# Centring the FFN matrix along its rows, taking the first normalisation's factors for two tiles at once, and moving the residual ahead of them on Pool

## The reference, cut to what matters

```
xn    = LN(x) * gamma + beta
gate  = sigmoid(xn @ w_gate + b_gate)
delta = sigmoid(xn @ w_delta + b_delta);   B = xn @ w_in + b_in
h_t   = tanh((h_{t-1} * delta_t) @ A + B_t)          # 2048 steps, state of 16
y     = (h @ C) * gate + x
x1    = LN(x + y)
out   = LN(x1 + real(ifft(fft(x1) @ w)) + bias)
```

## Time and profile before

| | us |
|---|---|
| median of three runs | 955.33 (955.02 to 956.43) |
| the profiled execution | 954.58 |
| its span, first to last instruction | 952.8 |
| PE busy | 919.6 (97%) |
| DVE busy | 755.5 (79%) |
| ACT busy | 561.2 (59%) |
| POOL busy | 515.0 (54%) |
| mean granted TensorE clock | 0.998 |

### The profile page before, as it was taken

One profiled execution on the slowest core, in us unless ns is written; L12 is line 12 of the kernel. 1 busy time (PEld: TensorE's weight loads), 2 busy tenths in 40 slices (PEclk: granted clock), 3 DMA queues, 4 the chain that ended last, 5 costly groups with the idle time before them and its releaser, 6 DMA issues.

```text
span 952.8 us, 19703 instructions
## 1 busy us (share of the span) xinstructions
PE 919.6 (97%) x5748; PEld 513.0 (54%) x5748; DVE 755.5 (79%) x1616; ACT 561.2 (59%) x1047; POOL 515.0 (54%) x1313
## 2 busy tenths in 40 slices
PE   6999999999999999999989999999999999999996
PEld 3555555555555555556775555454545454545453
DVE  6988788887888878888578887878787878787874
ACT  2533333333333333345474788888888888888887
POOL 1422222222222222232217888888888888888884
PEclk9999999999999999999999999999999999999999
DMA  9444455444554445532406576676766666767653
GB/s 328 137 141 146 156 176 176 137 149 155 176 176 137 147 157 176 176 133 93 174 1 174 179 248 233 223 244 223 235 222 240 224 238 221 238 225 239 223 176 133
DMA packets 89483, 175.84 MB, mean 185 GB/s; under 512 B 3057, under 2 KB 5361, under 8 KB 89458
## 3 DMA queue, kind: packets, MB, share of 16 engines
q1 hardware_dynamic: 89024, 175.00, 55.0%
q10 hardware_dynamic: 434, 0.54, 0.2%
HBM read 106.45 MB, written 67.11 MB: 182 GB/s over the span
## 4 chain that ended last, share of the span: by engine, by line
PE 48%; POOL 34%; issue 8%; DVE 5%; ACT 1%; DMA 1%; POOLq 1%; DVEq 0%
POOL x_sb L676 12%; PE bank L1164 12%; PE bank L1167 12%; PE bank L1165 12%; POOL rstd L634 7%; PE bank L1154 6%; POOL rnorm L700 4%; POOL scaled_mean L683 2%; POOL veps L632 2%; PE bank L1209 2%; PE bank L1188 1%; POOL lift_bias L686 1%; POOL rstd L702 1%; POOL nbias L704 1%; PE bank L1191 1%
## 5 line engine op out<-in xcount | busy, mean ns | idle before, releaser
L913 DVE SCALAR_TENSOR_TENSOR lo_sb<-bank,hi_sb 128x512 f16<-128x512 f32 x256 | 176.7, 690 | 84.0 <-ACT hi_sb L443 65.0
L443 ACT ACTIVATE hi_sb<-bank 128x512 f16<-128x512 f32 x128 | 76.4, 597 | 263.8 <-PE bank L1154 263.8
L632 POOL TENSOR_TENSOR veps<-mv,c_eps 128x1 f32<-128x1 f32 x256 | 49.4, 193 | 315.3 <-DVE mv L894 315.3
L1164 PE MATMUL bank<-z_sb,hi_sb 128*128 128x512 f16 x512 | 193.8, 379 | 9.3 <-DVE w_ring L1085 8.2
L1164 PE MATMUL bank<-wg_hi,hi_sb 128*128 128x512 f16 x512 | 194.0, 379 | 1.6 <-ACT hi_sb L443 0.8
L1165 PE MATMUL bank<-wg_lo,hi_sb 128*128 128x512 f16 x512 | 194.0, 379 | 0.0
L1165 PE MATMUL bank<-z_sb,hi_sb 128*128 128x512 f16 x512 | 193.9, 379 | 0.0
L676 POOL TENSOR_TENSOR x_sb<-x_sb,gate_sb 128x512 f32<-128x512 f32 x128 | 163.5, 1277 | 12.1 <-DVE gate_sb L1073 11.3
L1154 PE MATMUL bank<-cst,norm_sb 128*128 128x128 f32 x1024 | 158.7, 278 | 10.0 <-DVE norm_sb L907 8.2
L634 POOL TENSOR_TENSOR rstd<-veps,c_half 128x1 f32<-128x1 f32 x256 | 139.6, 545 | 20.1
L1079 DVE BATCH_NORM_STATS2 bn<-x_sb 128x6 f32<-128x512 f32 x128 | 88.5, 691 | 67.7 <-POOL x_sb L676 67.6
(11 more groups left out here) (158 smaller groups left out, 1215.9 us busy)
## 6 DMA issues: line engine op xcount, KB each, us to landing
x_sb<-x SPq DMA_DIRECT2D x63, 1024.0 KB, 6.9
gate_dram<-gate_sb SPq DMA_DIRECT2D x32, 1024.0 KB, 5.4
gate_sb<-gate_dram SPq DMA_DIRECT2D x32, 1024.0 KB, 5.3
out<-out_sb SPq DMA_DIRECT2D x31, 1024.0 KB, 5.3
h_rep<-fourier_constants SPq DMA_DIRECT2D x2, 514.0 KB, 12.8
x_sb<-x SPq DMA_DIRECT2D x2, 512.0 KB, 6.5
w_ring<-w_gate SPq DMA_DIRECT2D x2, 512.0 KB, 6.3
w_re_sb<-w_freq_real SPq DMA_DIRECT2D x1, 1024.0 KB, 12.2
```

The source lines that it names most:

```text
L913: nc.vector.scalar_tensor_tensor(lo_sb[:, k % 2].rearrange("p t r -> p (t r)"), ps_t[k % 2][:], ROW_SCALE, hi_sb[:, k % 2].rearrange("p t ...
L1164: nc.tensor.matmul(dst, hi_sb[:, k % 2, t], w_hi[:, t], start=(t == 0), stop=False)
```

## The change

M is centred along its rows: `combine` also takes the row sums of the last four tiles (two accumulators), makes from them `m_shift`, minus the row mean, and `high_m` and `low_m` add it. With such an M the FFN product of any row sums to zero, so the mean of `w_ring` is the mean of `norm_sb`, which is LIFT. `minus_mean`, `wsum` and `negmu` go; `squares` takes the constant -LIFT as its bias (both scaled by 1/sqrt(D)) and waits for `ffn_sum`; `scale_and_bias` has three instructions. The bound for M's scale is doubled. The first normalisation's factors are made for two tiles at once, in every odd slot, in two-column instructions, and the residual of n+5 stands ahead of them in POOL's slot.

```diff
@@ combine
+                if q < 2 * KT:
+                    ... (as before)
+                else:
+                    sums = m_sums[:, q - 2 * KT]
+                    nc.vector.scalar_tensor_tensor(dst[:, 0:HALF], odd[:, 0:HALF], ratio[sign], even, ALU.mult,
+                                                   ALU.add, accum_out=sums[:, 0:1])
+                    wait_own(nc.vector.scalar_tensor_tensor(
+                        dst[:, HALF:D], odd[:, HALF - 2:0:-1], ratio[-sign], even[:, HALF - 2:0:-1], ALU.mult,
+                        ALU.add, accum_out=sums[:, 1:2]))
+                    nc.vector.sem_inc(done, 1)
+                    nc.vector.tensor_scalar(m_shift[:, q - 2 * KT:q - 2 * KT + 1], sums[:, 0:1], sums[:, 1:2],
+                                            -1.0 / D, ALU.add, ALU.mult).then_inc(s_mshift, 1)
@@ high_m, low_m
-                act.wait_ge(s_pair, 2 * KT + i + 1)
-                nc.scalar.activation(m_hi[:, i], m_sb[:, i], ACT.Copy).then_inc(s_m_hi, 1)
+                act.wait_ge(s_mshift, i + 1)
+                nc.scalar.activation(m_hi[:, i], m_sb[:, i], ACT.Identity,
+                                     bias=m_shift[:, i:i + 1]).then_inc(s_m_hi, 1)
-                nc.vector.tensor_tensor(m_lo[:, i], m_sb[:, i], m_hi[:, i],
-                                        ALU.subtract).then_inc(s_msplit, 1)
+                nc.vector.scalar_tensor_tensor(m_lo[:, i], m_sb[:, i], m_shift[:, i:i + 1], m_hi[:, i], ALU.add,
+                                               ALU.subtract).then_inc(s_msplit, 1)
@@ ScalarE: b_normalise waits for the pair, squares for ffn_sum
-                act.wait_ge(s_blift, n + 1)
+                act.wait_ge(s_blift, v * 4 + k // 2 + 1)
-                act.wait_ge(s_negmu, n + 1)
+                act.wait_ge(s_w, n + 1)
-                nc.scalar.activation(gsum_sb[:, k % 2], w_ring[:, k], ACT.Square, bias=negmu[:, k:k + 1],
+                nc.scalar.activation(gsum_sb[:, k % 2], w_ring[:, k], ACT.Square, bias=c_squares[:],
+                                     scale=1.0 / float(np.sqrt(D)),
                                      accum_out=vsum[:, k:k + 1]).then_inc(s_sq, 1)
@@ GpSimd
+            def normalise_factors(m, k):
+                c = slice(k % 4, k % 4 + 2)
+                pool.wait_ge(s_baggr, m * 2 + 2)
+                pool.tensor_tensor(veps[:, c], mv[:, c, 1], c_eps4[:], ALU.add).then_inc(s_bveps, 1)
+                pool.wait_ge(s_bveps, m + 1)
+                pool.tensor_tensor(rstd[:, c], veps[:, c], c_half[:], ALU.pow).then_inc(s_brstd, 1)
+                pool.wait_ge(s_brstd, m + 1)
+                pool.tensor_tensor(scaled_mean[:, c], mv[:, c, 0], rstd[:, c], ALU.mult).then_inc(s_bmr, 1)
+                pool.wait_ge(s_bmr, m + 1)
+                pool.tensor_tensor(lift_bias[:, c], c_lift[:], scaled_mean[:, c],
+                                   ALU.subtract).then_inc(s_blift, 1)
-            def minus_mean(n, k):
...
@@ GpSimd, scale_and_bias
-                pool.tensor_tensor(rnorm2[:, c], var2[:, c], c_half[:], ALU.pow).then_inc(s_rnorm2, 1)
-                pool.wait_ge(s_rnorm2, m + 1)
-                pool.tensor_tensor(rstd2[:, c], rnorm2[:, c], c_rootd[:], ALU.mult).then_inc(s_rstd2, 1)
+                pool.tensor_tensor(rstd2[:, c], var2[:, c], c_half[:], ALU.pow).then_inc(s_rstd2, 1)
-                pool.tensor_tensor(nbias2[:, c], negmu[:, c], rstd2[:, c], ALU.mult).then_inc(s_nb2, 1)
+                pool.tensor_tensor(nbias2[:, c], c_neglift[:], rstd2[:, c], ALU.mult).then_inc(s_nb2, 1)
@@ GpSimd, slot of the second pass
-                if exists(n + 3):
-                    rstd_of(n + 3, (k + 3) % 8, s_baggr, s_bveps, s_brstd, c_eps4)
-                    lifted_bias(n + 3, (k + 3) % 8)
-                if exists(n - 2):
-                    minus_mean(n - 2, (k - 2) % 8)
                 if exists(n + 5):
                     residual(n + 5, (k + 5) % 8, v if k < 3 else v + 1)
+                if k % 2 == 1 and exists(n + 3):
+                    normalise_factors(v * 4 + (k + 3) // 2, (k + 3) % 8)
                 if k % 2 == 0 and exists(n - 4):
                     scale_and_bias(v * 4 + k // 2 - 2, (k - 4) % 8)
@@ VectorE
                 wait_own(nc.vector.tensor_reduce(bias_max[:], fbias_sb[:], AX.X, ALU.max, ...))
+                wait_own(nc.vector.tensor_scalar(bias_max[:], bias_max[:], 2.0, None, ALU.mult))
@@ ffn_sum
                 nc.vector.scalar_tensor_tensor(w_ring[:, k], ps_g[k % 2][:], unscale[:, 3:4],
-                                               norm_sb[:, k % 4], ALU.mult, ALU.add,
-                                               accum_out=wsum[:, k:k + 1]).then_inc(s_w, 1)
+                                               norm_sb[:, k % 4], ALU.mult, ALU.add).then_inc(s_w, 1)
```

More of the change, by code:

```diff
@@ L167, in build @@
         lift_bias = sb("lift_bias", [P, 4])
-        c_lift = sb("c_lift", [P, 1])
+        c_lift = sb("c_lift", [P, 2])
         c_eps = sb("c_eps", [P, 1])
-        c_eps4 = sb("c_eps4", [P, 1])
+        c_eps4 = sb("c_eps4", [P, 2])
         c_half = sb("c_half", [P, 2])
-        wsum = sb("wsum", [P, 8])
-        negmu = sb("negmu", [P, 8])
+        m_sums = sb("m_sums", [P, KT, 2])
+        m_shift = sb("m_shift", [P, KT])
+        c_neglift = sb("c_neglift", [P, 2])
+        c_squares = sb("c_squares", [P, 1])
         vsum = sb("vsum", [P, 8])
         var2 = sb("var2", [P, 8])
-        rnorm2 = sb("rnorm2", [P, 8])
         rstd2 = sb("rstd2", [P, 8])
-        c_mean = sb("c_mean", [P, 1])
-        c_epsd = sb("c_epsd", [P, 2])
-        c_rootd = sb("c_rootd", [P, 2])
+        c_eps2 = sb("c_eps2", [P, 2])
         nbias2 = sb("nbias2", [P, 8])
@@ L265, in build @@
         s_msplit = sem("m_split")
+        s_mshift = sem("m_centred")
         s_high = sem("scan_high_half")
@@ L295, in build @@
         s_w = sem("b_w")
-        s_negmu = sem("b_negmu")
         s_sq = sem("b_squares")
         s_var2 = sem("b_var2")
-        s_rnorm2 = sem("b_rnorm2")
         s_rstd2 = sem("b_rstd2")
@@ L580, in b_hi, with b_normalise @@
                                      scale=ROW_SCALE).then_inc(s_bhi, 1)
-            def b_normalise(n, k):
-                act.wait_ge(s_blift, n + 1)
+            def b_normalise(n, k, v):
+                act.wait_ge(s_blift, v * 4 + k // 2 + 1)
                 if before(n, 4):
@@ L608, in slot @@
                 if exists(n + 2):
-                    b_normalise(n + 2, (k + 2) % 8)
+                    b_normalise(n + 2, (k + 2) % 8, v if k < 6 else v + 1)
                 if exists(n - 5) and not (isinstance(n, int) and n - 5 == TILES - 1):
@@ L620, in _ @@
             pool.memset(c_eps4[:], LN_EPS / 4)
-            pool.memset(c_mean[:], -1.0 / D)
+            pool.memset(c_neglift[:], -LIFT)
+            pool.memset(c_squares[:], -LIFT / float(np.sqrt(D)))
             pool.memset(c_lift[:], LIFT)
-            pool.memset(c_epsd[:], LN_EPS * D)
-            pool.memset(c_rootd[:], float(np.sqrt(D)))
+            pool.memset(c_eps2[:], LN_EPS)
             pool.memset(c_half[:], -0.5).then_inc(s_pool_const, 1)
@@ L677, in residual @@
                                    gate_sb[:, k // 4, k % 4], ALU.add).then_inc(s_v, 1)
[L679 to L685, removed]
+            def normalise_factors(m, k):
[7 more added lines that the diff above has]
+                pool.wait_ge(s_bmr, m + 1)
                 pool.tensor_tensor(lift_bias[:, c], c_lift[:], scaled_mean[:, c],
                                    ALU.subtract).then_inc(s_blift, 1)
-            def minus_mean(n, k):
-                pool.wait_ge(s_w, n + 1)
-                pool.tensor_tensor(negmu[:, k:k + 1], wsum[:, k:k + 1], c_mean[:],
-                                   ALU.mult).then_inc(s_negmu, 1)
             def scale_and_bias(m, k):
@@ L697, in scale_and_bias @@
                 pool.wait_ge(s_sq, m * 2 + 2)
-                pool.tensor_tensor(var2[:, c], vsum[:, c], c_epsd[:], ALU.add).then_inc(s_var2, 1)
+                pool.tensor_tensor(var2[:, c], vsum[:, c], c_eps2[:], ALU.add).then_inc(s_var2, 1)
                 pool.wait_ge(s_var2, m + 1)
-                pool.tensor_tensor(rnorm2[:, c], var2[:, c], c_half[:], ALU.pow).then_inc(s_rnorm2, 1)
-                pool.wait_ge(s_rnorm2, m + 1)
-                pool.tensor_tensor(rstd2[:, c], rnorm2[:, c], c_rootd[:], ALU.mult).then_inc(s_rstd2, 1)
+                pool.tensor_tensor(rstd2[:, c], var2[:, c], c_half[:], ALU.pow).then_inc(s_rstd2, 1)
                 pool.wait_ge(s_rstd2, m + 1)
-                pool.tensor_tensor(nbias2[:, c], negmu[:, c], rstd2[:, c], ALU.mult).then_inc(s_nb2, 1)
+                pool.tensor_tensor(nbias2[:, c], c_neglift[:], rstd2[:, c], ALU.mult).then_inc(s_nb2, 1)
             def slot(n, k, v):
-                if exists(n + 3):
-                    rstd_of(n + 3, (k + 3) % 8, s_baggr, s_bveps, s_brstd, c_eps4)
-                    lifted_bias(n + 3, (k + 3) % 8)
-                if exists(n - 2):
```

(15 more changed lines are left out.)

## The result

The changed kernel takes 938.39 us (median of four runs, 938.24 to 939.56) against 955.17 for the kernel before (four runs, 954.54 to 956.43): ratio 0.983, 95% interval 0.9818 to 0.9841. 937.7 was forecast. Its profiled execution took 938.36 us with a span of 936.6, 16.2 less than before.

What follows compares the result with a forecast made beforehand. POOL was taken to bound the second pass after some ten tiles, with PE 5% below. Span 952.8 - 17.9 + 0.9 - 0.6 = 935.2, profiled execution 937.0, median 937.7 us; range 935 to 947.

Steps and rivals of the forecast that it cites:

- POOL 6.81 to 5.14 us a pair: Second pass: POOL's work per two tiles falls from 6.81 to 5.14 us, under PE's 6.49, so PE becomes the bound.
- Stalls of 17.9 us: Second pass, PE's first matmul of tile 0 to tile 127: 427.85 us, 410.0 without stalls; 17.9 is the most to gain.
- Rival A: Second pass: PE stalls remain in part, 0.15 us a pair over 64 pairs, 947 us; chance 0.14.
- The circle 6.27 + L: Second pass, four tiles: x load landing (L, 6.0 to 6.4), residual, factors, normalisations; 12.3 at L = 6.0, under PE's 12.97.
- Rivals B and C: Second pass, x load's landing bounds: B, L = 6.9, 944 us, chance 0.10; C, L = 7.6, 963 us, chance 0.03.
- The pair's wait has air: Second pass: paired factors wait for the later tile's variance; each step has more than 0.7 us of air.
- The end, -0.6: Behind the last matmul: negative mean with hand-over, one factor's step and an accumulator read go, -0.6 us.
- Between the passes, +0.9 (bounds -0.5 and +2): DVE's chain from scan's end to first FFN product: three combine at 0.3 more each, low_m may win or lose; +0.9 us.
- a first FFN matmul near 515.5: Start of the second pass on PE: a sign of the forecast being right; before it was 514.65.
- A slow `low_m` beside POOL: Between the passes: low_m took 1.12 us beside a POOL residual, 0.68 ahead of one; each of four may shift 0.44.
- 0.75 above it: Last step of the sum: median of the runs taken 0.75 us above the profiled execution, 937.0 to 937.7.

Runs made afterwards that it cites:

- extra transfer: Changed kernel with a 512 KB copy within DRAM, never read, issued ahead of each load of x in the second pass: 991.09 us, ratio 1.0368.
- factors ahead: Changed kernel with two calls swapped, so the paired first factors stand before the residual in POOL's slot: 980.93 us, ratio 1.0276.
- centring alone: Changed kernel with M centred, but first factors one tile at a time and ahead of the residual, as before: 939.26 us, ratio 0.9838.
- filled: The zero frequency kernel with nine unused matmuls in PE's gap between the passes: 936.26 us, ratio 0.9797.
- pairs alone: Kernel before with paired factors, the residual ahead of them, minus_mean first in the slot, M not centred: 937.54 us; again 936.58 us.
- zero frequency: Changed kernel, but M centred by clearing column 0 of both frequency weights and the bias's mean in the first pass: 936.13 us; again 936.24 us.
- both added powers: Two runs: changed kernel with one or two more unused two-column powers per pair on POOL: 939.36 us with one, 942.0 us with two.

## Why the prediction was right, step by step

- *POOL 6.81 to 5.14 us a pair.* Measured 5.15. The strided two-column add takes 0.20 and its step 0.27, as taken. From 560 to 900 POOL was busy 251.6 of 340 us, 26% idle by busy time (hand-overs are not busy) and 21% by steps; some 20% was said.
- *Stalls of 17.9 us, all of them removable.* 409.95 for 410.0. Rival A (0.15 a pair, 947) did not happen: no wait of PE for `w_ring` is left.
- *The circle 6.27 + L with L of 6.0 to 6.4.* Landing was 5.8 at least, 6.0 in the median, 6.3 at most, with the store 2.4 ahead (2.6 said) and the gate load 3.17 behind (3.0 said). POOL waited 55.7 us for it and ACT 1.1 for POOL: by 6.27 + 6.0 against 12.97 the air is 0.7 a quad. Rivals B and C stay rivals of another landing time; the extra transfer shows the circle, with its sign, and its constant right to 0.1 us.
- *The pair's wait has air.* Only the order makes it so: factors ahead cost 42 us against the changed kernel.
- *The end, -0.6.* -0.54.
- *Between the passes, +0.9 (bounds -0.5 and +2).* The one term that was mis-sized: +2.24, outside its bounds, the failed step of the sum. The sign that hung on it, a first FFN matmul near 515.5, failed with it (516.89). Counted from `flag`, so without what lies before it, the cost is 16.03 - 14.41 = 1.62, inside the bounds; the second profile of the changed kernel has 2.34, centring alone 1.73. Where the 2.24 lies:
  - 0.62 stands before `flag` (500.86 for 500.24). Over the kernels here `flag` came from 500.16 to 501.34 (filled, extra transfer), and kernels with the same stretch before it differ as much (500.24 before, 501.06 pairs alone), so this is no cost of the centring that the runs show.
  - 1.49 is on DVE's chain from `flag` to the transposes of tile 0 (12.04 for 10.55). Three `combine` cost 0.40 each, not 0.3. One of them in the changed kernel:

```profile
510.24 0.42 DVE L996 SCALAR_TENSOR_TENSOR out_sb<-bank,even_sb 128x257 f32<-128x257 f32 x1
510.58 0.09 DVE L996 DVE_READ_ACCUMULATOR out_sb<-bank,even_sb 128x1 f32 x1
...
510.93 0.09 DVE L998 DVE_READ_ACCUMULATOR out_sb<-bank,even_sb 128x1 f32 x1
511.17 0.21 DVE L1002 TENSOR_SCALAR m_shift<-m_sums 128x1 f32<-128x1 f32 x1 [0.16 <-DVE out_sb L998]
511.30 0.68 DVE L1084 BATCH_NORM_STATS2 bn<-x_sb 128x6 f32<-128x512 f32 x1
```

  - That is 1.06 us from the first to the statistics, for 0.66 before. The accumulators' rows cost little; the wait of an instruction for the one just ahead of it, 0.16 idle with its hand-over, and the tiny instruction make the rest. `low_m` as a three-operand instruction takes 0.74 for 0.68, twice on the chain: 0.12. 0.16 is a longer idle time ahead of the first `gated` (0.46 for 0.30) that the profile puts down to nothing; its cause stays open. 1.20 + 0.12 + 0.16 = 1.48.
  - The last 0.13 is from the transposes to the first product (3.99 for 3.86), with the clock at half, which the prediction did not think of. The clock costs more there than 0.13: the 3.86 before hold a wait of 0.50 for `gated`, the 3.99 hold none. The longer chain made one gap of PE 1.70 us long where 1.13 had been the longest:

```profile
510.83 0.38 PE L1312 MATMUL bank<-w_ring,h_lo 128*128 128x512 f16 x1
512.90 1.11 PE L1158 MATMUL bank<-cst,norm_sb 128*128 128x128 f32 x4 [1.70 <-ACT norm_sb L586]
```

- *A slow `low_m` beside POOL.* The price fell on the other side. All four `low_m` took 0.74, none 1.12 as in the earlier trace rows. Instead three of POOL's first five residuals took 1.70 to 1.71 for 1.27, each with a `low_m` running beside it (504.29, 508.13 and 512.78), where one of the first six before did (1.65). Two of them:

```profile
508.29 1.70 POOL L676 TENSOR_TENSOR x_sb<-x_sb,gate_sb 128x512 f32<-128x512 f32 x1 [0.91 <-DVE gate_sb L1078]
...
512.94 1.71 POOL L676 TENSOR_TENSOR x_sb<-x_sb,gate_sb 128x512 f32<-128x512 f32 x1 [0.21 <-DVE gate_sb L1078]
```

The Trainium skill (SBUF — State Buffer, Who interferes with whom) has it that the one that starts second is blocked. The trace agrees: these residuals began 0.16 us behind a `low_m` and lost 0.43, and the `low_m` lost nothing by them.

The total came within 0.7 us although one term was 1.3 off, and this part is luck: the median of the runs lay level with the profiled execution and not 0.75 above it. The mechanism is no luck: the 17.9 us of stalls went as forecast, against 16.2 gained in all.

## What to carry to other kernels

Compute each engine's step per pair and stop when the next bound is passed: here either half of the change was enough, and the half that needed no work on the path between the passes was 2 us better (936.6, with pairs alone, against 938.55) than the whole; clearing the zero frequency early (936.2) does the same for the centring. Before you batch an instruction over two items, look what is queued behind its longer wait on that engine, and whether the thing waited for depends on it: the same instructions in the other order cost 42 us. An instruction moved on an in-order engine moves the releases of everything behind its reader too: the order alone, which moved `minus_mean` behind the residual and the residual ahead of the factors, cost 13 us, and because it moved both the run does not share them out. Move one thing at a time.

## What the runs showed of the hardware

- The granted clock fell to 0.50, the 1.2 GHz level, within 2 us behind an idle time of PE of 1.70 us, in both profiles of the changed kernel and in the five other profiles that have this idle time (centring alone, factors ahead, extra transfer, both added powers; 1.69 in one). With idle times of 1.13 and 0.74 us it fell in two profiles (zero frequency) and stayed at 1.00 in two (before, pairs alone), so the idle times alone do not decide; with 1.13 and 1.51 (the order alone) it fell; with the gap filled it stayed, in the one profile there is. At the lower level FFN matmuls stood 0.43 us apart, not 0.216, as here in the changed kernel's second run:

```profile
517.60 0.63 PE L1168 MATMUL bank<-z_sb,hi_sb 128*128 128x512 f16 x1
518.03 0.63 PE L1169 MATMUL bank<-z_sb,hi_sb 128*128 128x512 f16 x1
```

- A two-column power on POOL costs 0.65 us where nothing waits for it and 0.78 as a step in a chain of semaphores; an add or subtract on two columns takes 0.15 (717.56 to 717.71) and 0.27 (716.23 to 716.50).
